# Router of the first 2048 tokens in a pause between two steps of attention, and most of their dispatches in attention's later steps

## The chip, the cores and the metric

The kernel runs on one core of a Trainium2 chip. The metric is the device time of one execution in microseconds (us); lower is better. Engines are named as in the profile: PE (TensorE matmul; PEld its weight loads), DVE (VectorE), ACT (ScalarE), POOL (GpSimd), SP (SyncE, which here only issues DMAs). A DMA that POOL issues with a list of row addresses appears as DMA_INDIRECT on POOL itself.

## The reference, cut to what matters

One transformer block over x of 4 x 1024 x 128 (4096 tokens, in the kernel 32 tiles of 128 tokens) with a modulation by batch:

```python
h = _layernorm(x) * (1 + ca) + sa
x = x + ga * attention(h)            # 16 heads of 8, scores kept where |q - k| <= half, half <= 60
h = _layernorm(x) * (1 + cb) + sb
score = relu(h @ rw1 + rb1) @ rw2 + rb2          # router: 128 -> 512 -> 8
_, topi = top_k(score, 2)                        # two of eight experts for each token
gate = softmax(where(mask(topi), score, -inf))
out = sum over e of gate[:, e] * (relu(h @ W1[e] + b1[e]) @ W2[e] + b2[e])
x = x + gb * out
```

Attention of a tile needs only keys within 60 tokens of it. Everything behind attention is done token by token.

## The kernel before, in words

The program is written out for each engine by hand; every engine runs its own list in order and waits on semaphores. There is no scheduler.

**Preparation** (0 to 43 us): first layer norm, modulation, projections q, k, v.

**Attention** (43 to 255 us) runs 32 steps, one for each tile of 128 tokens. A step has four groups of scores. For each group PE makes the scores (`scores`, L1055), DVE takes row maxima (`maxima`, L1093), ACT takes exponentials (L1026, four per group, each with a read of its sum) and DVE transposes them (`turn`, L1101; the last group's transpose, `turn_last`, L925, stands in the next step). PE then multiplies with the values (`weighted`, L899), one step behind. POOL's list for step t (`turn` in `attend_gpsimd`) is: half of the spread queries of step t + 2 (`queries`, qbd, L338), the spread of the softmax denominators (`denominators`, rsp, L937), the other half of the queries, and the residual sum of the tile before (`residual`, xg L868 and x_all L872). DVE takes the moments of the finished tile for the second layer norm (`moment`, `aggregated`). From step 12 on POOL also refines 1/sqrt(var) of a finished batch of eight tiles by Newton steps (`refined`) and modulates its rows (`group_modulated`, four operations for a group of four tiles, result in h_all).

**Router** (255 to 330 us). The tokens form eight groups of 512 (`NG`). For each group PE turns the rows (`turned_rows`, L1478), makes four hidden blocks (`hidden`, L1485), four partial score products (`partial`, L1492) and their sum (`summed`, L1500). ACT copies and rectifies between them (`turned` L1537, `rectified` L1549, `partials` L1543). DVE adds the bias (`token_scores`, L1425), picks two experts (`choose_both`, 12 operations) and turns ranks into places (`place`), after PE has counted the tokens before each (`ranked`, L1508 and L1510). Choice and places go by parts of tiles, `PARTS = ((0, 4), (4, 8), (8, 16), (16, 24), (24, 32))`. At the head of this stage DVE refines and modulates what POOL hasn't: `last_refined` for the last batch and `last_modulated` for groups 6 and 7.

**Dispatch.** For each tile and each of the two choices POOL issues one DMA_INDIRECT that writes the 128 rows of h_all (576 bytes each) to their places in a DRAM tensor xs, sorted by expert (`dispatch`, L1614): 64 in all, each followed by a small MEMSET on POOL (`breath`, L1656). The last part's dispatches alternate with scatters, two to one.

**Experts** (330 to 513 us) run 72 tiles of 128 sorted rows. DVE builds four lists of which rows and which expert a tile has (`listed`, lists of tiles 0 to 7, 8 to 23, 24 to 39, 40 to 71). SP loads a tile's rows (hg, L1584) once its list stands and all dispatches of batches up to the list's number have landed (`d_x[k]`). PE transposes them (L1927), multiplies up (L1935) and down (L1943); DVE copies weights and rows (`first_matrix` L1793, `gathered` L1798, L1801) and adds the bias (`result`, ys, L1809); ACT rectifies (L1700); POOL scatters the result rows back to token order (`scatter`, L1647). In turns 0 to 5 DVE also has list 2 and the last part's choice; in turns 10 to 15 list 3.

**End** (513 to 537 us): the two results of each token are fetched, weighted, added and stored.

What sets the order around the change is the order of the text in these functions:

```python
                for t in range(NT):           # attend_gpsimd
                    turn(t)
                    ...
                    if t >= 1:
                        residual(e, (t - 1) // 2, (t - 1) % 2)
                sent = 0                      # route_gpsimd
                for p, (first, end) in enumerate(PARTS):
                    routed(e, p)
                    for r in range(2 * first, 2 * end):
                        dispatch(e, r // 2, r % 2)
                        breath()
```

## Time and profile before

| | |
|---|---|
| median of 3 runs | 537.14 us (531.41 to 538.80) |
| profiled execution | 538.34 us, its span 536.5 us |
| PE busy | 453.1 us (84% of the span) |
| DVE busy | 378.4 us (71%) |
| POOL busy | 369.7 us (69%) |
| ACT busy | 349.0 us (65%) |
| mean granted clock of TensorE | 0.927 |

The profile is of one execution. About 1.8 us of its time lie outside the span. All stage times below are us from the span's start. A busy share is an average over stages that have different limits: what a change in one stage is worth is read from that stage.

### The profile page before, as it was taken

To read this page: it belongs to the slowest core of one execution; us is meant where nothing else is said; L and a number is where in the kernel's file an instruction comes from. 1 tells how busy PE (TensorE), PEld (TensorE's weight loads), DVE (VectorE), ACT (ScalarE), POOL (GpSimd) and SP (SyncE) were. 2 spreads that over 40 slices of the span, in tenths; PEclk is the share of its full clock that TensorE was granted. 3 is DMA by queue.
4 is the path that set the end of the run, shared out by engine and by line. 5 is a ranking of instruction groups with operands and counts; after the bars stand their busy time and mean duration, and the time that the engine had idled before them with its cause. 6 is when DMAs were issued, how large, how long until landed. Compare 5 with 4: busy or idle time off the path is not lost.

```text
span 536.5 us, 16755 instructions
## 1 busy us (share of the span) xinstructions
PE 453.1 (84%) x5323; PEld 356.0 (66%) x5323; DVE 378.4 (71%) x1026; ACT 349.0 (65%) x1521; POOL 369.7 (69%) x586
## 2 busy tenths in 40 slices
PE   6998888888888888887929996659668999999977
PEld 5565666666666666665504446658447999999977
DVE  6777999999999999999493565735332554555654
ACT  3668999999999999999523552424023787756800
POOL 6975655556688668764447879875888877777640
PEclk9999999999999999999876996969557999999979
DMA  9351000000000400301311121222211222224446
GB/s 236 83 172 46 13 12 13 13 12 13 14 13 12 111 14 14 91 12 44 99 44 34 51 83 51 81 70 79 91 60 61 80 71 82 69 81 137 133 135 194
DMA packets 61519, 36.54 MB, mean 68 GB/s; under 512 B 25806, under 2 KB 57334, under 8 KB 61306
## 3 DMA queue, kind: packets, MB, share of 16 engines
q1 hardware_dynamic: 55834, 25.83, 18.4%
q0 software_dynamic: 4352, 9.45, 5.2%
q8 instruction: 45, 0.74, 0.6%
q10 hardware_dynamic: 1248, 0.20, 0.2%
q14 instruction: 40, 0.33, 0.2%
HBM read 20.56 MB, written 14.88 MB: 66 GB/s over the span
## 4 chain that ended last, share of the span: by engine, by line
PE 35%; DVE 22%; ACT 21%; issue 12%; another core or an unknown queue 5%; POOL 2%; DVEq 2%; ACTq 0%; POOLq 0%
ACT pr L1026 20%; PE pAm L1935 9%; DVE nmax L1093 8%; PE pAm L1485 5%; PE pSpm L1943 5%; PE pScm L1943 4%; PE pScm L1255 2%; DVE oT L947 1%; PE pScm L1500 1%; DVE w1t L1793 1%; DVEq L1552 1%; PE pm L767 1%; DVE stat L1337 1%; PE pSpm L1492 1%
## 5 line engine op out<-in xcount | busy, mean ns | idle before, releaser
L1026 ACT ACTIVATE pr<-pS,nmax 128x136 f32<-128x136 f32 x512 | 185.5, 382 | 13.4 <-DVE nmax L1093 13.2
L1700 ACT ACTIVATE act<-pAm,w1t 128x128 f32<-128x128 f32 x288 | 82.6, 377 | 85.4 <-PE pAm L1935 41.2
L1026 ACT ACTIVATION_READ_ACCUMULATOR pr<-pS,nmax 128x1 f32 x512 | 108.8, 212 | 0.0
L1935 PE MATMUL pAm<-hgT,w1t 128*128 128x128 f32 x576 | 87.2, 293 | 19.3 <-issue 12.8
L1055 PE MATMUL pS<-kT,qbd 64*128 64x136 f32 x1024 | 93.8, 302 | 1.5 <-ACT pr L1026 1.2
L1935 PEld LDWEIGHTS pAm<-hgT,w1t 128*128 128x128 f32 x576 | 77.6, 206 | 24.7 <-issue 20.0
L1647 POOL DMA_INDIRECT y_scr<-ys,si x72 | 73.2, 1016 | 29.7 <-DVE ys L1809 18.0
L1093 DVE TENSOR_REDUCE nmax<-pS 128x4 f32<-128x544 f32 x128 | 87.6, 685 | 2.1 <-PE pS L1059 1.4
L1101 DVE STREAM_TRANSPOSE prT<-pr 128x640 f32<-128x640 f32 x96 | 81.1, 845 | 8.9 <-ACT pr L1026 0.2
L1055 PEld LDWEIGHTS pS<-kT,qbd 64*128 64x128 f32 x1024 | 68.3, 186 | 14.6 <-ACT pr L1026 1.1
L1614 POOL DMA_INDIRECT xs<-h_all,pos_i x64 | 64.0, 999 | 11.3 <-issue 9.6
L338 POOL TENSOR_TENSOR qbd<-qT,eqd 128x512 f32<-128x512 f32 x64 | 67.6, 1059 | 1.0 <-issue 0.2
L937 POOL TENSOR_TENSOR rsp<-rden,eqt 128x256 f32<-128x256 f32 x33 | 20.5, 621 | 64.4 <-DVE rden L931 61.4
L899 PE MATMUL pO<-prT,vbd 128*32 128x32 f32 (+3 forms) x2048 | 62.4, 253 | 0.0
L899 PEld LDWEIGHTS pO<-prT,vbd 128*32 128x32 f32 x2048 | 47.1, 146 | 19.6 <-issue 19.2
L1793 DVE COPY w1t<-w_all 128x644 f32 x72 | 40.4, 561 | 20.4 <-issue 10.4
L1656 POOL MEMSET unread<- 128x240 f32 x128 | 45.7, 357 | 0.1
L1943 PE MATMUL pScm<-w_all,act 128*128 x288 | 42.1, 285 | 3.7 <-issue 3.3
L1943 PE MATMUL pSpm<-w_all,act 128*128 x288 | 42.2, 289 | 1.6 <-issue 1.6
L920 PE MATMUL pRF<-wcg,oT 128*128 128x128 f32 x68 | 16.5, 324 | 29.4 <-DVE oT L947 28.6
L1943 PEld LDWEIGHTS pScm<-w_all,act 128*128 128x128 f32 x288 | 37.5, 200 | 4.8 <-issue 4.8
L1943 PEld LDWEIGHTS pSpm<-w_all,act 128*128 128x128 f32 x288 | 38.0, 202 | 3.4 <-issue 3.4
(304 smaller groups left out, 716.4 us busy)
## 6 DMA issues: line engine op xcount, KB each, us to landing
hg<-xs SPq DMA_DIRECT2D x72, 72.0 KB
vbd<-v_scr SPq DMA_DIRECT2D x132, 16.0 KB, 1.7
v_scr<-h_all SPq DMA_DIRECT2D x8, 256.0 KB, 2.3
h_all<-y_scr SPq DMA_DIRECT2D x8, 256.0 KB, 3.1
w_all<-y_scr SPq DMA_DIRECT2D x8, 256.0 KB, 5.0
x_all<-in_L_attn_x SPq DMA_DIRECT2D x3, 512.0 KB, 6.1
w_all<-in_L_ffn_W SPq DMA_DIRECT2D x2, 768.0 KB, 4.9
w_all<-in_L_ffn_W SPq DMA_DIRECT2D x3, 512.0 KB, 5.1
```

Source lines behind the costliest of these rows:

```text
L338: e.tensor_tensor(qbd[u][:, 4 * a:4 * a + 4, :].rearrange("p q (h t) -> p q h t", h=NH8), qT[:, bass.ds(t * P + 4 * a * QT, 4 * QT)].rearr ...
L899: mm = e.matmul(pO[32 * hg:32 * hg + 32, lo * QB:(hi + 1) * QB], strided(values, hg, [[HG, QB]]), strided(prT[w][:, hg // 2, 0:1], 2 * WIN ...
L1026: e.activation(pr[:, n, to:to + SPAN], scored(j, gi)[:, lo:lo + SPAN], ACT.Exp, bias=nmax[:, k:k + 1], scale=-1.0, accum_out=rs[u][:, k:k ...
L1055: e.matmul(scored(j, gi)[:, n * BANK + f * SPAN:n * BANK + (f + 1) * SPAN], qbd[j % RING][of_head, 2 * gi + f, :], kT[of_head, first:first ...
L1093: e.tensor_reduce(strided(nmax[:, 0:1], 2 * gi, [[QN, 2], [1, 2]]), strided(scored(j, gi)[:, 0:1], 0, [[BANK, 2], [SPAN, 2], [1, SPAN]]), ...
L1101: e.transpose(rows_of(prT[u], gi), rows_of(pr, gi)).then_inc(v_tr.sem, 1)
L1614: e.indirect_dma_start(out=xs, out_offset=bass.IndirectOffsetOnAxis(ap=pos_i[:, k, n:n + 1].bitcast(U32), axis=0), in_=h_all[:, n, :], in_ ...
L1647: e.indirect_dma_start(out=y_scr, out_offset=bass.IndirectOffsetOnAxis(ap=si[:, j:j + 1].bitcast(U32), axis=0), in_=ys[j % R // 2][:, j % ...
L1700: e.activation(ac(u)[:, k, :], pU[u % W][:, k, :], ACT.Relu, bias=w1t[u // 2 % 4][:, u % 2, FF + D + k:FF + D + k + 1]).then_inc(a_up.sem, 1)
L1793: e.tensor_copy(w1t[u // 2 % 4][:, u % 2, :], w1_all[:, bass.ds(x_, 1), :].rearrange("p a f -> p (a f)")).then_inc(v_w.sem, 1)
L1935: mm = e.matmul(pU[u % W][:, k, :], w1t[u // 2 % 4][:, u % 2, k * P:(k + 1) * P], hgT[u // 2 % 4][:, u % 2, :], start=True, stop=True)
L1943: mm = e.matmul(pY[u // 2 % 2][:, u % 2, 0:D], ac(u)[:, k, :], w2_all[:, bass.ds(x_ * FF + k * D, D)], start=k == 0, stop=k == FC - 1)
```

## The change

The router of groups 0 to 3 (tiles 0 to 15, `G1 = 4`) is taken out of the router stage and put ahead of attention step 20 (`FIRST = NT // 2 + 4`) on PE, ACT, DVE and POOL. Since the buffers of the router stage don't exist during attention, these groups use halves of kT and qT, and staging tiles of the preparation, and another PSUM bank for their scores. Parts 0 to 2 are chosen and placed there; the ranking of part 2 follows on PE behind step 20. POOL issues 28 of these tiles' 32 dispatches inside its turns 20 to 31: three a turn up to turn 27, one a turn from 28 on, without breaths. The last four, and those of parts 3 and 4, stay behind attention. Refinement of batches 1 and 2 moves from POOL to DVE (`batch_refined`, between steps). POOL modulates groups 2 and 3 in the pause and groups 4 and 5 in turns 28 to 31. Behind attention DVE makes lists 0 and 1 before it takes the scores of group 4. The last part is ranked in turn 5 of the experts and not 9, and list 3 follows in turns 6 to 11. Two scatters come ahead of the last part's dispatches. Weight loads on SP wait until the pause's last partial product.

```diff
+            FIRST = NT // 2 + 4
                     if s in LOADED:
+                        e.wait_ge(t_sp, G1)
                         load_weights(e, *LOADED[s])
+                def send(t, k):
+                    if t < FIRST or sent[0] == NT or k and t >= NT - 4:
+                        return
+                    if sent[0] == 2 * PARTS[NP1 - 1][0]:
+                        routed(e, NP1 - 1)
+                    dispatch(e, sent[0] // 2, sent[0] % 2)
+                    sent[0] += 1
                     denominators(e, t // 2, t % 2)
+                    send(t, 0)
                     if t + 2 < NT:
                         queries((t + 2) // 2, t % 2, t + 2, 1)
+                    send(t, 1)
                 for t in range(NT):
+                    if t == FIRST:
+                        first_half_gpsimd(e)
                     turn(t)
...
                         residual(e, (t - 1) // 2, (t - 1) % 2)
+                    send(t, 2)
+                    if t >= NT - 4:
+                        e.wait_ge(v_gs, 3)
+                        for k in range(2 * (t - NT + 4), 2 * (t - NT + 5)):
+                            group_modulated(e, 4 + k // 4, k % 4)
                     if n >= 0 and n % TPB == TPB - 1:
+                        if n // TPB in (1, 2):
+                            batch_refined(e, n // TPB)
                         kept(e)
                         e.sem_inc(v_gs, 1)
+                    if 2 * i + u == FIRST:
+                        summed(e, G1 - 1)
+                        e.wait_ge(v_rt, NP1 - 1)
-            RANKED = 9
+            RANKED = 5
+            SOON = 2
-            BEHIND = {0: 6, 5: 8, 6: 10, 7: 12}
+            BEHIND = {0: 6}
+            def first_half_tensor(e):
+                i, u = (FIRST - 1) // 2, (FIRST - 1) % 2
+                e.wait_ge(d_rw, 64)
+                e.wait_ge(v_k, 3)
+                a_e.wait(e, i, u)
+                turned_rows(e, 0)
+                v_o.wait(e, i, u)
+                a_r.wait(e, i, u)
+                a_x.wait(e, i, u, back=1)
+                for g in range(G1):
+                    group_of_router(e, g, 0, G1)
+                partial(e, G1 - 1)
+            def first_half_vector(e):
+                token_scores(e, 0)
+                choose_both(e, 0)
+                token_scores(e, 1)
+                place(e, 0)
+                choose_both(e, 1)
+                token_scores(e, 2)
+                place(e, 1)
+                token_scores(e, 3)
+                choose_both(e, 2)
+            def first_half_gpsimd(e):
+                e.wait_ge(v_gs, 2)
+                for k in range(8):
+                    group_modulated(e, 2 + k // 4, k % 4)
+                routed(e, 0)
+                routed(e, 1)
+                for r in range(NT - 4, NT):
+                    dispatch(e, r // 2, r % 2)
+                    breath()
-                for p, (first, end) in enumerate(PARTS):
+                for p in range(NP1, len(PARTS)):
-                token_scores(e, 0)
-                choose_both(e, 0)
-                place(e, 0)
-                token_scores(e, 1)
-                choose_both(e, 1)
-                place(e, 1)
                 all_listed(0)
-                token_scores(e, 2)
-                token_scores(e, 3)
-                choose_both(e, 2)
+                all_listed(1)
                 token_scores(e, 4)
-                place(e, 2)
-                all_listed(1)
```

PE's list between steps 19 and 20 (pO<-prT are the products with the values, pS the scores, pRF<-wcg the projection). Before:

```order
L899 MATMUL pO<-prT,vbd 32x64 x4
L899 MATMUL pO<-prT,vbd 32x32 x4
L1055 MATMUL pS<-kT,qbd 128x136 x4
L1059 MATMUL pS<-masks,rep 128x272 x2
L920 MATMUL pRF<-wcg,oT 128x128
```

With the change, from the end of step 19 to the first rows of group 0's router, where the remaining 30 rows follow:

```order
L902 MATMUL pO<-prT,vbd 32x64 x4
L902 MATMUL pO<-prT,vbd 32x32 x4
L1538 MATMUL pTm<-ident,h_all 128x128 x8
L1545 MATMUL pAm<-modr,rw_sb 128x512 x4
L1538 MATMUL pTm<-ident,h_all 128x128 x4
L1545 MATMUL pAm<-gated,rw_sb 128x512 x2
L1552 MATMUL pSpm<-kT,rw2p 32x512 x4
```

and from its last partial product into step 20:

```order
L1552 MATMUL pSpm<-qT,rw2p 32x512 x4
L1083 MATMUL pS<-kT,qbd 128x136 x4
L1087 MATMUL pS<-masks,rep 128x272 x2
L1560 MATMUL pXm<-sel,scp_w 128x8 x4
L923 MATMUL pRF<-wcg,oT 128x128
```

Four router groups now stand between two rows that followed each other; nothing of step 20 stands among them but its first group of scores.

POOL's list for one late turn, from denominators to the next denominators. Before, turn 27 (L338 queries, L868 and L872 residual):

```order
L937 TENSOR_TENSOR rsp<-rden,eqt 128x256
L338 TENSOR_TENSOR qbd<-qT,eqd 128x512
L868 TENSOR_TENSOR xg<-x_all,gacv_bc 128x128
L872 TENSOR_TENSOR x_all<-xg,xa 128x128
L338 TENSOR_TENSOR qbd<-qT,eqd 128x512
L937 TENSOR_TENSOR rsp<-rden,eqt 128x256
```

With the change, turns 20 to 27:

```order
L940 TENSOR_TENSOR rsp<-rden,eqt 128x256
L1723 DMA xs<-h_all,pos_i 34816x144
L340 TENSOR_TENSOR qbd<-qT,eqd 128x512
L1723 DMA xs<-h_all,pos_i 34816x144
L871 TENSOR_TENSOR xg<-x_all,gacv_bc 128x128
L875 TENSOR_TENSOR x_all<-xg,xa 128x128
L1723 DMA xs<-h_all,pos_i 34816x144
L340 TENSOR_TENSOR qbd<-qT,eqd 128x512
```

One dispatch now stands behind the denominators, one behind the queries and one behind the residual.

## Rows read from the trace of the kernel before

**Rows 1.** Busy time by stage (stretch, length, then engines, PEclk, DMA share, GB/s)
```profile
43.20:254.90 211.70, 181.04 (x3458) 132.21 (x3456) 201.12 (x378) 198.14 (x1090) 138.28 (x222) 1.00 0.13 27
254.90:329.80 74.90, 58.50 (x327) 30.38 (x325) 43.78 (x169) 31.18 (x51) 51.62 (x77) 0.82 0.20 61
329.80:420.00 90.20, 67.23 (x412) 59.61 (x413) 38.96 (x145) 29.88 (x108) 73.72 (x113) 0.75 0.24 72
420.00:500.00 80.00, 80.00 (x720) 80.00 (x719) 43.47 (x127) 56.38 (x201) 60.08 (x87) 1.00 0.34 99
```

**Rows 2.** Timeline at the router's start (start, duration, engine, line, operation, [idle before])
```profile
254.56 1.09 PE L1478 MATMUL pTm<-ident,h_all 128*128 128x128 f32 x4
...
255.69 0.60 ACT L1537 ACTIVATE h2T<-pTm 128x512 f32<-128x512 f32 x1 [0.74 <-PE pTm L1478]
```

**Rows 3.** Timeline, PE's rows of two router groups in sequence
```profile
298.43 1.06 PE L1492 MATMUL pSpm<-act,rw2p 128*32 128x512 f32 x8
...
299.42 1.99 PE L1485 MATMUL pAm<-h2T,rw_sb 128*128 128x512 f32 x4
...
302.54 0.95 PE L1500 MATMUL pScm<-sel,scp 128*128 128x8 f32 x8
...
304.38 1.06 PE L1492 MATMUL pSpm<-act,rw2p 128*32 128x512 f32 x8
```

**Rows 4.** Timeline, DVE: first and last operation of list 0; of a choice
```profile
294.42 0.16 DVE L1733 TENSOR_TENSOR cnt<-run,basec 128x8 f32<-128x8 f32 x1
...
299.18 0.17 DVE L1783 TENSOR_TENSOR used<-used,most 128x8 f32<-128x8 f32 x1
...
315.97 0.22 DVE L1437 TENSOR_REDUCE m<-score 128x8 f32<-128x64 f32 x1
...
318.81 0.23 DVE L1452 TENSOR_TENSOR ohb<-oh 128x64 bf16<-128x64 f32 x1
```

**Rows 5.** Timeline, DVE's refinement and modulation at the router's start, beside POOL
```profile
264.47 0.68 DVE L1399 TENSOR_SCALAR var<-mv 128x8 f32<-128x8 f32 x1
...
268.69 1.29 POOL L1391 TENSOR_TENSOR h_all<-h_all,modbc 128x512 f32<-128x512 f32 x1
...
268.87 1.13 DVE L1406 TENSOR_TENSOR newt<-newt,var 128x8 f32<-128x8 f32 x1
...
279.04 0.69 DVE L1421 TENSOR_TENSOR h_all<-h_all,modbc 128x512 f32<-128x512 f32 x1
```

**Rows 6.** Timeline, PE's long wait and the end of the router
```profile
282.64 0.21 PE L1508 MATMUL pXm<-ohb,upper 128*128 128x32 bf16 x1 [10.90 <-DVE ohb L1452]
...
282.80 2.06 PE L1485 MATMUL pAm<-h2T,rw_sb 128*128 128x512 f32 x2
...
326.07 0.19 DVE L1425 TENSOR_TENSOR score<-pScm,rb_bc 128x32 f32<-128x32 f32 x1
...
329.79 3.62 PE L1935 MATMUL pAm<-hgT,w1t 128*128 128x128 f32 x16 [2.81 <-DVE hgT L1798]
```

**Rows 7.** Timeline of POOL: a modulation inside turn 26; turn 27 and the next denominators
```profile
219.91 1.27 POOL L1393 TENSOR_TENSOR h_all<-h_all,modbc 128x512 f32<-128x512 f32 x1
...
222.47 0.62 POOL L937 TENSOR_TENSOR rsp<-rden,eqt 128x256 f32<-128x256 f32 x1 [0.27 <-DVE rden L931]
...
229.35 0.62 POOL L937 TENSOR_TENSOR rsp<-rden,eqt 128x256 f32<-128x256 f32 x1 [3.18 <-DVE rden L931]
```

**Rows 8.** Timeline of POOL, dispatches behind attention
```profile
385.15 0.97 POOL L1614 DMA_INDIRECT xs<-h_all,pos_i  x1 [0.17 <-issue]
...
386.61 0.98 POOL L1614 DMA_INDIRECT xs<-h_all,pos_i  x1 [0.16 <-issue]
```

**Rows 9.** Timeline of the experts while POOL dispatches
```profile
375.67 0.47 PE L1943 MATMUL pSpm<-w_all,act 128*128 x2 [0.37 <-issue]
...
395.70 0.42 DVE L1809 TENSOR_TENSOR ys<-pSpm,w1t 128x256 f32<-128x256 f32 x1 [13.33 <-remote]
```

**Rows 10.** DMA queues, 372 to 402 us (queue, kind: packets, MB, share)
```profile
q8 instruction: 1, 0.02, 0.2%
```

More of the change, by code:

```diff
@@ L190, in build @@
         ohb = [sb(f"ohb{p}", [P, end - first, NE], BF16) for p, (first, end) in enumerate(PARTS)]
-        run = sb("run", [P, NE])
+        run = [sb(f"run{p}", [P, NE]) for p in range(len(PARTS))]
         posg = sb("posg", [P, TPB, NE])
@@ L1044, in scores @@
                         e.wait_ge(a_k, NG)
+                    if 2 * i + u == FIRST and gi < NS:
+                        first_half_left(e, (HG * j + gi) % NS)
                     if gi >= NS:
@@ L1132, in attend_vector @@
                 for t in range(NT):
+                    if t == FIRST:
+                        first_half_vector(e)
                     step(t // 2, t % 2, t % SPANS)
+                    if t == FIRST:
+                        place(e, NP1 - 1)
                     between(t)
@@ L1279, in pPre_of, with pSc_of, h2T_of, scp_of @@
             def pPre_of(p):
-                bank = pX if p < len(PARTS) - 1 else pSc
+                bank = pX if NP1 <= p < len(PARTS) - 1 else pSc
                 place_of = bank[:, 0, P:P + (TPB + 1) * NE]
                 return place_of.rearrange("p (t k) -> p t k", k=NE)
+            def pSc_of(g):
+                return whole(pX if g < G1 else pSc)
+            def h2T_of(g):
+                return ((modr_w, gated_w) if g < G1 else h2T)[g % 2][:, :]
+            def scp_of(g):
+                return ((wmod_sb, scp_w) if g < G1 else scp)[g % 2][:, 0:GRP]
+            def act_of(g):
+                if g < G1:
+                    return (kT, qT)[g % 2][:, 0:FC * GRP].rearrange("p (k t) -> p k t", k=FC)
+                return act[g % 2][:, :, :]
             def modulated_rows(e, g):
@@ L1484, in hidden @@
                     e.wait_ge(a_a2, FC * (g - 1) + k + 1)
-                e.matmul(whole(pA[k]), rw1_sb[:, k * P:(k + 1) * P], h2T[g % 2][:, :], start=True, stop=True).then_inc(t_a2, 1)
+                e.matmul(whole(pA[k]), rw1_sb[:, k * P:(k + 1) * P], h2T_of(g), start=True, stop=True).then_inc(t_a2, 1)
             def partial(e, g):
@@ L1491, in partial @@
                 for k in range(FC):
[L1492 removed]
+                    mm = e.matmul(whole(pSp)[QB * k:QB * k + QB, :], rw2p[:, k, :], act_of(g)[:, k, :], start=True, stop=True, skip_group_check=True)
                 mm.then_inc(t_sp, 1)
@@ L1499, in summed @@
                 for n in range(4):
-                    mm = e.matmul(whole(pSc)[:, n * NE:(n + 1) * NE], scp[g % 2][:, n * P:(n + 1) * P], sel[:, :], start=True, stop=True)
+                    mm = e.matmul(pSc_of(g)[:, n * NE:(n + 1) * NE], scp_of(g)[:, n * P:(n + 1) * P], sel[:, :], start=True, stop=True)
                 mm.then_inc(t_sc, 1)
@@ L1512, in ranked, with group_of_router @@
                 mm.then_inc(t_rk, 1)
-            def group_of_router(e, g):
-                if g + 1 < NG:
+            def group_of_router(e, g, first, end):
+                if g + 1 < end:
                     turned_rows(e, g + 1)
                 hidden(e, g, 0)
-                if g >= 4:
-                    summed(e, g - 2)
-                if g == 6:
-                    ranked(e, 2)
                 hidden(e, g, 1)
-                if g >= 1:
+                if g > first:
                     partial(e, g - 1)
-                if g in (2, 3):
+                if first == 0 and g >= 2:
@@ new lines, in first_half_left, with first_half_scalar @@
+            def first_half_left(e, bank):
+                if bank == 0:
+                    e.wait_ge(a_t2, G1)
+                    e.wait_ge(v_sc, G1)
+                else:
+                    e.wait_ge(a_a2, FC * G1)
+            def first_half_scalar(e):
+                turned(e, 0)
+                for g in range(G1):
+                    if g + 1 < G1:
+                        turned(e, g + 1)
+                    rectified(e, g, 0)
+                    rectified(e, g, 1)
+                    if g >= 1:
+                        partials(e, g - 1)
+                    rectified(e, g, 2)
+                    rectified(e, g, 3)
+                partials(e, G1 - 1)
@@ L1536, in turned @@
                     e.wait_ge(t_a2, FC * (g - 1))
-                e.activation(h2T[g % 2][:, :], whole(pT), ACT.Copy).then_inc(a_t2, 1)
+                e.activation(h2T_of(g), whole(pT), ACT.Copy).then_inc(a_t2, 1)
             def partials(e, g):
@@ L1542, in partials @@
                     e.wait_ge(t_sc, g - 1)
-                e.activation(scp[g % 2][:, :], whole(pSp), ACT.Copy).then_inc(a_sp, 1)
+                e.activation(scp_of(g), whole(pSp), ACT.Copy).then_inc(a_sp, 1)
             def rectified(e, g, k):
@@ L1548, in rectified @@
                 e.wait_ge(t_a2, FC * g + k + 1)
-                e.activation(act[g % 2][:, k, :], whole(pA[k]), ACT.Relu, bias=rb1_sb[:, k:k + 1]).then_inc(a_a2, 1)
+                e.activation(act_of(g)[:, k, :], whole(pA[k]), ACT.Relu, bias=rb1_sb[:, k:k + 1]).then_inc(a_a2, 1)
             def expert(e, i, u):
@@ L1631, in route_gpsimd @@
                 residual(e, NI, 0)
-                for k in range(2, 8):
-                    group_modulated(e, 4 + k // 4, k % 4)
                 v_tr.wait(e, NI - 1, 1)
@@ L1657, in breath @@
                     breaths[0] += 1
+                for r in range(NT - 4, NT):
+                    dispatch(e, r // 2, r % 2)
+                    breath()
                 sent = 0
-                for p, (first, end) in enumerate(PARTS):
+                for p in range(NP1, len(PARTS)):
+                    first, end = PARTS[p]
+                    if p == len(PARTS) - 1:
+                        for _ in range(SOON):
+                            scatter(sent)
+                            breath()
+                            sent += 1
                     routed(e, p)
@@ L1677, in route_scalar @@
                 projected(e, NI, 0)
-                turned(e, 0)
+                turned(e, G1)
                 to_rows(e, NI, 0)
-                for g in range(NG):
+                for g in range(G1, NG):
                     if g + 1 < NG:
```

50 lines of the change are left out of this document (30 added, 20 removed).

## The prediction

> **What bounds the kernel now.** The table of busy time by stage comes first [rows 1]; its columns after the length are PE, PEld, DVE, ACT, POOL, clock, DMA share and GB/s. In attention DVE and ACT are busy 201 and 198 of 212 us, so its 32 steps of 6.6 us have no hole for anything on these two. POOL has one: 138 of 212. A turn of POOL, seen in its timeline, ends 3.2 us before the next denominators are due [rows 7]: 6.88 us from one rsp to the next, of which 3.7 are work. The router stage has no full engine (58 of 75 on PE). It is a chain, and its worst link is one wait of PE of 10.9 us for the choice on DVE [rows 6]. In the experts PE sets the pace where all goes well: 720 rows in the 80 us from 420 on, 9.0 a us, none idle. Ahead of that, 329.8 to 420, it did 412 rows in 90.2 us [rows 1]. At 9.0 a us they take 45.8 us, so **44 us are lost there**. About 7 belong to turns 0 to 5, in which DVE also has list 2 and the last choice (about 1.2 each). The other 37 are stalls: two PE products that took 0.47 us after 0.37 idle on "issue", where the good stretch has nine rows a us, and DVE rows that waited 13.3 us for a signal from elsewhere [rows 9]. All this lies where POOL issues indirect DMAs every 1.46 us (385.15 to 386.61, of which the DMA_INDIRECT is 0.97 and the rest a small MEMSET and gaps [rows 8]).
>
> The sum is made against the profiled execution (538.3 us, 1.2 above the median).
>
> **(a) The pause, +34.** From the last exponential of step 19 to the first of step 20, ACT does only router work and DVE too. In order: PE turns group 0 and ACT copies it, 1.7 us (254.56 to 256.29 [rows 2]). The eight products of its hidden blocks take 4.0 (1.99 for four [rows 3]). Group 2 must wait for its modulation: DVE's refinement of batch 1 is 14 operations of 0.17 and a gap, 2.9; POOL's four operations of 1.27 [rows 7] make 5.1 more. That is 8.0 against 5.7 on PE, so 2.3 of wait. Three groups more at the period of the old stage, 298.43 to 304.38 or 5.95 [rows 3], are 17.9. Parts 0 and 1 are ranked in it (0.9). The last partial and its copy are 2.4, the sum 1.0 [rows 3]. Part 2's choice has 3.1 (315.97 to 319.04 [rows 4]), the score ahead of it 0.2. Step 20's first maxima, 0.7, end it. Together 34.2. The maxima of step 20 stand behind all of DVE's choice in the order of its list, so no part of the choice is hidden. Bounds: 31, if the modulation is early and choice overlaps; 45, if the clock is at its lower level for the pause, where two products take 2.06 in place of 1.0 [rows 6, 3].
>
> **(b) The router behind attention, -28.** Before it was 74.9 (254.9 to 329.8 [rows 1]). Now only groups 4 to 7 are left, and groups 4 and 5 are modulated in turns 28 to 31. DVE starts its refinement at 264.5 as before, since the last residual sets that. It took 8.9 us up to 273.3, as some operations of 0.17 took 1.13 while POOL modulated beside them [rows 5]. POOL now has nothing there: I take 5. The modulation of group 6 is four of 0.69, 2.8, so PE may turn it at 272.3, and group 7 is done at 275.1. Then DVE makes lists 0 and 1, 4.9 each (294.42 to 299.35 [rows 4]), and takes the scores of group 4 at about 285.2. PE has gone on to group 6 and waits there for that read. From it there are two periods of 5.95 and a ranking to the last scores at 297.4. The old kernel needed 3.7 from its last scores to the first product of an expert (326.07 to 329.79 [rows 6]); with place 3 a bit more, 4.3. The experts start 301.7 on the old scale, 46.8 behind attention: -28. Bounds -25 (refinement as slow as before) and -31 (lists partly beside PE's work of group 6).
>
> **(c) Attention's later steps, +8.** In turns 20 to 27 POOL has 3.65 of its own and three dispatches of 0.97 with a gap of 0.17 [rows 8], 3.45: 7.1 a turn against steps of 6.6. That is +0.5 for eight turns, 4, less about 1 of slack at the start: +3. What is late then is the spread of softmax denominators; ACT and DVE wait for the products behind them. The refinement of batch 2 now lies on DVE, which is full there: +3 to 4 (2.9 alone; 8.9 beside POOL's reads [rows 5]). Turns 28 to 31 have one dispatch and two modulation rows of 1.27: 3.65 + 1.15 + 2.5 = 7.3, +1.2 in all after slack. Bounds: 0 (the denominators absorb it, as 3.2 us idle stood there [rows 7]) and +20 (below).
>
> **(d) The experts, -6.** Before they took 183: 139 at PE's pace and 44 lost. Turns 0 to 5 cost the same 7; list 3 comes in turns 6 to 11, where before the stalls hid it: 4. The stalls I tie to the time in which POOL issues indirect DMAs without a pause beside the experts. Before this was about 78 us, and cost 37: 0.47 a us. Now part 3 is sent from 298 to 322 and part 4 with its scatters to 360: 58 us, which gives 27. I take 26. The sum is 139 + 7 + 4 + 26 + 1 for the two scatters = 177. Bounds: 0 for the stalls, -32; 37 as before, +5. Lists don't gate: tile 24 isn't due before 349, and the last dispatch lands by 360.
>
> **Sum:** 538.3 + 34 - 28 + 8 - 6 = 546.3; less 1.2 to the median, **545 us**. The pause buys back nearly its price and no more: the same four groups cost 34 in a place where all else stands still, and save 28 in the other. The gain can come from the experts alone, with 28 of the 64 dispatches gone from there.
>
> **Rivals.**
>
> *B, faster: the stalls go.* If the loss of 37 comes from dispatches that gate loads (SP waits for a whole batch before it may load hg, then all arrive together) rather than from POOL's pace, it goes with the 28 dispatches. For it: it ended at about 416, some 15 us behind the last dispatch, and batch 3 landed last at 401. Against: PE rows of a tile whose data were there also crept [rows 9]. With 5 left in place of 26 the time is 524; with 0, 519. Place it at 521. Chance 0.28.
>
> *C, slower: the stalls move into attention.* 28 dispatches of 1.15 are 32 us of POOL's issuing. At the same 0.47 lost for each such us, attention loses 15 more than POOL's own time, since DVE and ACT have no slack [rows 1]: 560. It decides from +3: a turn from 20 to 27 of over 7.5 us. Against: the dispatches behind denominators, queries and residual are apart, so POOL does not issue them back to back. Chance 0.15.
>
> *D, slower: the clock.* PE stood 10.9 us and its products came at 2.06 for two afterwards [rows 6]; the stage has a mean clock of 0.82, attention 1.00 [rows 1]. In the pause PE waits 2 to 3 us at three places. At the lower level (1.2 GHz) for half of it, 555. Chance 0.05.
>
> *E, slower: the stall is tied to a place in the program.* PE creeps with "issue" as the releaser, as if its instructions came late. Then it recurs at the same tiles with all its 37: 556. Against: the queue that brings instructions had a single packet in these 30 us [rows 10]. Chance 0.07.
>
> The Trainium skill (Runtime: NRT & Kernel Launch, section Instruction fetch mechanics) says that an engine's instructions are fetched in blocks of 16 KiB while it works through the last, and that the cost is mostly hidden; the one packet agrees, and by that page E would add nothing. The Trainium skill (SBUF — State Buffer, section Who interferes with whom) says that a VectorE operation with two inputs in SBUF and a GpSimd operation that reads SBUF exclude each other; by that, batch 2's refinement in the middle of attention could cost up to the slow case. The trace agrees in 264 to 273, where only some of the operations were slow.
>
> **Chances and range.** The forecast has 0.45, with a range of its own of 538 to 552: pause 31 to 37, attention +3 to +12, stalls 18 to 33. A change under 2% is about what a measurement of this kernel can't tell from none: 526.4 to 547.9. Of the forecast's 0.45, 0.34 lie within, 0.11 above. B gives 0.24 to faster and 0.04 to within. C, D and E give 0.25 to slower and 0.02 to within. Faster 0.24, within 0.40, slower 0.36. The range that holds 8 in 10 is 520 to 564: below it lies half of B, above it the far end of C.
>
> **What would show it.** Right: ACT's gap between steps 19 and 20 about 34; rsp to rsp in turns 20 to 27 about 7.1; first L1935 row (new line number) 47 behind attention's end; the clock at 1.00 in the pause; PE rows of the first 60 us of the experts at less than 9 a us and "issue" among their releasers, ending with the last dispatch. Wrong: stalls gone with POOL still dispatching (B); turns 20 to 27 at 7.5 or more (C); a lower clock in the pause (D); the stall at the same tiles as before (E).

## Result, and the profile of the changed kernel

| | before | changed |
|---|---|---|
| median, four runs each | 534.27 us (531.28 to 538.80) | 555.79 us (550.69 to 557.04) |
| profiled execution, its span | 538.34, 536.5 | 555.90, 554.1 |
| ratio | | 1.038 (95% interval 1.027 to 1.049) |
| mean granted clock | 0.927 | 0.911 |

The changed kernel is slower by 3.8%. The forecast was 545 us. Its wide range of 520 to 564 holds the result, its own range of 538 to 552 does not, and the likeliest case (within 2%) did not come. Busy time by stage, changed kernel (stretch, length, then PE, PEld, DVE, ACT, POOL, clock, DMA share, GB/s), to set beside [rows 1]. The stretches are all attention with its pause, the pause, steps 20 to 31, the router behind attention, the experts' first 79 us, a later stretch of the experts:

```profile
48.70:306.00 257.30, 215.85 (x3584) 150.61 (x3581) 218.28 (x461) 214.33 (x1112) 169.11 (x234) 0.95 0.12 30
176.00:214.00 38.00, 32.19 (x224) 16.84 (x216) 15.93 (x74) 19.57 (x47) 12.32 (x16) 0.91 0.13 37
214.00:306.00 92.00, 73.95 (x1276) 53.67 (x1277) 81.07 (x164) 75.31 (x408) 75.89 (x93) 0.89 0.18 48
306.00:351.60 45.60, 31.33 (x196) 15.86 (x196) 27.55 (x114) 16.38 (x27) 14.60 (x24) 0.80 0.23 66
351.60:431.00 79.40, 62.89 (x337) 54.02 (x338) 34.11 (x133) 22.28 (x81) 58.31 (x91) 0.73 0.23 69
431.00:500.00 69.00, 69.00 (x622) 69.00 (x621) 37.39 (x109) 50.74 (x182) 51.13 (x74) 1.00 0.26 76
```

The pause fills PE to 32 of 38 us, DVE and ACT only to 16 and 20. In steps 20 to 31 no engine is over 81 of 92, where DVE was at 95% over all of attention before. The experts are as before: 9.0 PE rows a us in the good stretch, 337 rows in 79 us ahead of it. By marks that both timelines have (first exponential; denominators of steps 0, 19, 20 and the last; first expert product; last ys; end), the two executions split so:

| part | before | changed | difference | forecast |
|---|---|---|---|---|
| preparation, to the first exponential | 44.6 | 49.9 | +5.3 | none |
| steps 0 to 19 | 125.0 | 124.9 | -0.1 | 0 |
| denominators 19 to 20 (the pause) | 6.9 | 40.3 | +33.4 | +34 |
| denominators 20 to the last | 79.1 | 91.9 | +12.8 | +8 |
| to the first expert product | 74.2 | 44.7 | -29.5 | -28 |
| experts, to the last ys | 185.0 | 181.8 | -3.2 | -6 |
| end | 21.7 | 20.7 | -1.0 | 0 |

The sum is +17.6 (before rounding), that of the two spans.

**The pause.** ACT's last exponential of step 19 and first of step 20, and on DVE the first score, the last choice and the maxima behind it:

```profile
179.55 0.38 ACT L1050 ACTIVATE pr<-pS,nmax 128x136 f32<-128x136 f32 x1
...
214.16 0.37 ACT L1050 ACTIVATE pr<-pS,nmax 128x136 f32<-128x136 f32 x1 [5.31 <-DVE nmax L1131]
```
```profile
193.33 0.19 DVE L1485 TENSOR_TENSOR score<-pXm,rb_bc 128x32 f32<-128x32 f32 x1 [10.74 <-PE pXm L1560]
...
210.06 0.19 DVE L1485 TENSOR_TENSOR score<-pXm,rb_bc 128x32 f32<-128x32 f32 x1 [3.91 <-PE pXm L1560]
...
213.33 0.16 DVE L1513 TENSOR_TENSOR gates<-m 128x8 f32<-128x8 f32 x1
213.41 0.72 DVE L1131 TENSOR_REDUCE nmax<-pS 128x4 f32<-128x544 f32 x1
```

Four scores at 193.3, 199.4, 205.3 and 210.1: twice the period of 6 us from [rows 3], then 4.8. The last exponential and the next are 34.6 us apart.

**Turns 20 to 27.** POOL from one denominators row to the next:

```profile
239.21 0.62 POOL L940 TENSOR_TENSOR rsp<-rden,eqt 128x256 f32<-128x256 f32 x1
240.00 1.01 POOL L1723 DMA_INDIRECT xs<-h_all,pos_i  x1 [0.17 <-issue]
241.04 1.06 POOL L340 TENSOR_TENSOR qbd<-qT,eqd 128x512 f32<-128x512 f32 x1
242.26 1.01 POOL L1723 DMA_INDIRECT xs<-h_all,pos_i  x1 [0.17 <-issue]
243.30 0.46 POOL L871 TENSOR_TENSOR xg<-x_all,gacv_bc 128x128 f32<-128x128 f32 x1
243.93 0.46 POOL L875 TENSOR_TENSOR x_all<-xg,xa 128x128 f32<-128x128 f32 x1 [0.17 <-POOL xg L871]
244.60 0.99 POOL L1723 DMA_INDIRECT xs<-h_all,pos_i  x1 [0.22 <-PE pS L1087]
245.62 1.07 POOL L340 TENSOR_TENSOR qbd<-qT,eqd 128x512 f32<-128x512 f32 x1
246.64 0.62 POOL L940 TENSOR_TENSOR rsp<-rden,eqt 128x256 f32<-128x256 f32 x1
```

No gap over 0.22 is left and the denominators wait for nothing, where 3.18 us stood idle before [rows 7]: POOL sets 7.43 us a turn. In turn 21, of 8.98 us, PE's granted clock falls to 0.50 for 4 us, and POOL waits 1.52 us for the denominators; eight score products take 1.28 there and 0.73 later:

```profile
223.68 1.28 PE L1083 MATMUL pS<-kT,qbd 64*128 64x136 f32 x8
...
228.35 0.73 PE L1083 MATMUL pS<-kT,qbd 64*128 64x136 f32 x8
```
```profile
222.80:227.00 4.20, 4.20 (x64) 3.07 (x64) 2.95 (x4) 3.01 (x17) 3.81 (x6) 0.50 0.05 18
```

Turn 25 takes 8.11 at full clock. In it POOL turns part 2's places into addresses (`routed`), 0.69 us more with the gaps, which no term of the sum had:

```profile
257.01 0.21 POOL L1730 TENSOR_SCALAR h_all<-rank 128x8 f32<-128x8 f32 x1
257.28 0.20 POOL L1731 CAST pos_i<-pos 128x16 int32<-128x16 f32 x1
257.76 1.03 POOL L1723 DMA_INDIRECT xs<-h_all,pos_i  x1 [0.28 <-POOL pos_i L1731]
```
```profile
254.10:262.10 8.00, 5.77 (x110) 4.17 (x110) 6.44 (x13) 6.43 (x36) 6.93 (x10) 1.00 0.16 38
```

Turn 26, where the mean clock is 0.68, still takes 7.41: there POOL hides it.

Turn 27, with the refinement of batch 2 on DVE in it, takes 10.82. POOL waits for it:

```profile
273.89 0.28 DVE L1459 TENSOR_SCALAR var<-mv 128x8 f32<-128x8 f32 x1
...
275.41 1.66 DVE L1464 TENSOR_TENSOR newt<-rstd 128x8 f32<-128x8 f32 x1
...
278.32 0.17 DVE L1470 TENSOR_TENSOR rstd<-rstd,newt 128x8 f32<-128x8 f32 x1
...
280.39 0.62 POOL L940 TENSOR_TENSOR rsp<-rden,eqt 128x256 f32<-128x256 f32 x1 [3.35 <-DVE rden L934]
```

**The preparation.** Its text is the same in both kernels, up to line numbers. One DVE row with two inputs in SBUF, of one element, stood 4.64 us. It started while the second of POOL's four queries rows ran and ended with the fifth row from there, at 38.3. PE then waited 2.68 us, and its clock fell (0.52 from 39.4 to 42.0, 1.00 in the same place before):

```profile
32.57 4.10 POOL L340 TENSOR_TENSOR qbd<-qT,eqd 128x512 f32<-128x512 f32 x4
...
33.67 4.64 DVE L389 TENSOR_TENSOR sc<-sc 1x1 f32<-1x1 f32 x1
...
37.84 0.46 POOL L636 TENSOR_TENSOR wcg<-modbc,wc 128x128 f32<-128x128 f32 x1
...
39.43 1.12 PE L756 MATMUL pQ<-h_all,wqs 128*128 128x512 f32 x1 [2.68 <-DVE qT L396]
```

**The experts.** Late signals are still there (rows of ys that waited 8.83 and 10.45 us on "remote", to set beside [rows 9]), now at the first and at the fifth to seventh ys row (one for two tiles); before it was the sixth to ninth.

```profile
412.06 0.42 DVE L1925 TENSOR_TENSOR ys<-pScm,w1t 128x256 f32<-128x256 f32 x1 [8.83 <-remote]
...
425.32 0.42 DVE L1925 TENSOR_TENSOR ys<-pSpm,w1t 128x256 f32<-128x256 f32 x1 [10.45 <-remote]
```

What the 28 early dispatches leave free on POOL turns into waiting. POOL stands 22.88 us before part 3 for its places and 9.00 before part 4 for its:

```profile
347.60 0.21 POOL L1730 TENSOR_SCALAR h_all<-rank 128x8 f32<-128x8 f32 x1 [22.88 <-DVE pos L1531]
...
385.53 0.20 POOL L1730 TENSOR_SCALAR h_all<-rank 128x8 f32<-128x8 f32 x1 [9.00 <-DVE pos L1531]
```

In the kernel before it had no wait at part 3 and 6.54 at part 4. Part 4's last dispatch moved from 400.0 to 419.1.

### The profile page after: what moved, and what is told of

It is laid out like the page before. It is cut to its first block, busy times and chain, and to the rows that moved or that the text cites. A ratio compares the mean times of both kernels' runs of the same rounds, so it can differ in the third digit from the quotient of the medians.

```text
span 554.1 us, 16734 instructions
## 1 busy us (share of the span) xinstructions
PE 466.7 (84%) x5323; PEld 363.2 (66%) x5323; DVE 381.2 (69%) x1054; ACT 350.2 (63%) x1521; POOL 354.4 (64%) x530
## 4 chain that ended last, share of the span: by engine, by line
PE 41%; ACT 18%; DVE 17%; issue 11%; POOL 7%; another core or an unknown queue 4%; DMA 1%; DVEq 1%; SPq 0%; ACTq 0%; POOLq 0%
ACT pr L1050 15%; PE pAm L2041 10%; DVE nmax L1131 5%; PE pAm L1545 5%; PE pScm L2049 5%; PE pSpm L2049 5%; POOL xs L1723 2%; PE pS L1083 2%; PE pO L902 2%; ACT act L1816 2%; PE pScm L1300 2%; POOL qbd L340 2%; PE pSpm L1552 1%; DMA x_all<-in_L_attn_x 1%
## 5 line engine op out<-in xcount | busy, mean ns | idle before, releaser
L2041 PE MATMUL pAm<-hgT,w1t 128*128 128x128 f32 x576 | 90.5, 298 | 13.2 <-issue 6.2
L1083 PE MATMUL pS<-kT,qbd 64*128 64x136 f32 x1024 | 98.0, 312 | 1.5 <-ACT pr L1050 1.2
L2041 PEld LDWEIGHTS pAm<-hgT,w1t 128*128 128x128 f32 x576 | 79.2, 208 | 19.5 <-issue 14.6
L1083 PEld LDWEIGHTS pS<-kT,qbd 64*128 64x128 f32 x1024 | 71.6, 194 | 16.4 <-ACT pr L1050 1.9
L902 PE MATMUL pO<-prT,vbd 128*32 128x32 f32 (+3 forms) x2048 | 64.7, 259 | 6.5 <-DVE prT L928 6.5
L902 PEld LDWEIGHTS pO<-prT,vbd 128*32 128x32 f32 x2048 | 48.6, 147 | 27.4 <-issue 26.8
L923 PE MATMUL pRF<-wcg,oT 128*128 128x128 f32 x68 | 17.2, 336 | 24.9 <-DVE oT L950 22.7
L1087 PE MATMUL pS<-masks,rep 64*128 64x272 bf16 x256 | 37.1, 282 | 0.0
```

Source lines behind the costliest of these rows:

```text
L902: mm = e.matmul(pO[32 * hg:32 * hg + 32, lo * QB:(hi + 1) * QB], strided(values, hg, [[HG, QB]]), strided(prT[w][:, hg // 2, 0:1], 2 * WIN ...
L1083: e.matmul(scored(j, gi)[:, n * BANK + f * SPAN:n * BANK + (f + 1) * SPAN], qbd[j % RING][of_head, 2 * gi + f, :], kT[of_head, first:first ...
L2041: mm = e.matmul(pU[u % W][:, k, :], w1t[u // 2 % 4][:, u % 2, k * P:(k + 1) * P], hgT[u // 2 % 4][:, u % 2, :], start=True, stop=True)
```

## Experiments

One thing has to be known first: the same kernel before has a median of 534.4 us beside one group of runs and of 514.6 and 514.7 beside the two others. The twelve runs came in three groups of four, each group on a chip of its own, and each run is compared with the kernel before of its own group. Each chip was met only once, so what belongs to the chip and what to its condition at that time can't be told apart. In the two groups at 515 no trace has a DVE row that waited over 1.5 us on "remote"; in the group at 534, and in the two first profiles, all have them. I call these a **quiet** and a **stalling** chip. On a quiet chip the kernel before has times and no trace, and the changed kernel has neither as it stands.

**Both kernels again, for traces beside each other** (a stalling chip). No edit.

> The kernel before, unchanged, for a trace on this chip. On the chip of the last four runs its median was 514.6 us, against 537.1 where both were profiled first. If the stalls of the experts belong to the chip or its moment and not to the program, its trace there has no DVE row that waits over 2 us on a late signal, and PE does its 9 rows a us from about 380 on; at the end POOL's scatters, spaced 1.46 us by the MEMSETs, are the last to finish. If they belong to the program, the stretch 372 to 418 creeps here too. Ratio to itself 1.00.

> The changed kernel, unchanged. From its parts: pause 34, router behind attention 29 shorter, last twelve steps 12 longer, so 17 behind at the first expert; without stalls, POOL's chain of dispatches and scatters sets the end, and it has 28 fewer of them behind attention. Theory POOL (the end is POOL's, no stalls): the experts take 5 to 12 us less than in the kernel before, 520 to 527 where before is 515. Theory stalls (the experts' loss is as on the first chip): 533 to 556.

Measured: 533.4 against 534.4 for the kernel before, ratio 0.999 (0.996 to 1.002), and 548.9 for the changed one, ratio 1.027 (1.019 to 1.035). The parts repeat: first exponential 44.3 and 49.2; pause 39.9 between denominators; from denominators 20 to the last 79.0 and 91.9; the router behind attention 74.4 and 44.7; experts 178.4 and 177.5. The change gives the experts 1 to 3 us on a stalling chip and not 6. The text for the stalling case (533 to 556) holds the changed kernel.

**No dispatch in attention, and two a turn** (a quiet chip).

```diff
 def send(t, k):
-    if t < FIRST or sent[0] == NT or k and t >= NT - 4:
+    if True:
```

with all 32 dispatches behind attention, and for two a turn, with twelve behind it

```diff
+    if t < FIRST or sent[0] == NT or k == 2 or k and t >= NT - 4:
```

> The changed kernel, but with no dispatch inside attention: all 32 of tiles 0 to 15 are issued behind it. My theory from the two traces: POOL's turns 20 to 27 set the 7.4 us steps, so the last twelve steps come back from 91.8 us (first to last denominators of turns 20 to 32) to about 83, with only the refinement of batch 2 above the old 79.1. Behind attention 28 dispatches of 1.46 us are added ahead of part 3, whose first dispatch then stands some 50 us behind attention and not 43; the experts lose about as much to stalls as before (35 to 40 us) instead of 30. Sum: 556 - 9 + 7 = about 554, no clear difference from the changed kernel. Rival B (dispatches in attention are what helps the experts): above 562. Rival C (dispatches in attention cost more than the turns): below 547.

> The changed kernel with two dispatches a turn in turns 20 to 27 and not three; 20 go in attention, 12 behind. My theory: POOL has 3.65 + 2 x 1.18 = 6.0 a turn, under the 6.57 of DVE and ACT, so the turns fall back to 6.6 us and attention gets 7 us shorter, for 8 more dispatches behind it that are hidden (part 3 isn't chosen before 43 us behind attention): 549. Rival: the turns stay near 7.4, since a dispatch delays the denominators wherever it stands: 556.

The numbers of these two expectations are for a chip like that of the first profiles; what holds here is their distances. Measured: 537.9 with none, ratio to the kernel before 1.046 (1.040 to 1.053); 519.0 with two a turn, 1.009 (1.005 to 1.013). From denominators 20 to the last it is 83.9 us with none, 85.2 with two, 91.7 with three (on a quiet chip, next but one below). So in attention the third dispatch costs 6.5 us and the first two 1.3: it is the length of POOL's turn that counts, not the dispatch. (The kernel with three is the repaired one at the end of this section; its whole time, 518.8, is that of the kernel with two, whose preparation was 2.6 us longer in its trace.) Of the run with none I expected no clear difference to the changed kernel, and that was wrong: it is the slowest of these, though its attention is the shortest. The rival of that text, that the dispatches in attention are what helps the experts, is the one that this chip bears out. Its part 4 starts at 383.1 and not at 370.4, and POOL then never catches up: the last ys stands at 500.1, POOL's last scatter 13.6 us behind it.

DVE's last ys row, and POOL's last row:

```profile
500.07 0.41 DVE L1926 TENSOR_TENSOR ys<-pScm,w1t 128x256 f32<-128x256 f32 x1
```
```profile
513.67 0.97 POOL L1754 DMA_INDIRECT y_scr<-ys,si  x1 [0.30 <-issue]
```

In this run the end belongs to POOL's chain of dispatches and scatters, one each 1.46 us at best, and dispatches taken out of its head are worth their time: with two a turn part 4 starts at 366.0, 17.2 us sooner, and the span is 17.4 shorter.

**The kernel before without the MEMSETs, twice** (both times a quiet chip). `breath()` returns at once.

> The kernel before without any of the small MEMSETs, so dispatches follow at 1.15 us. Theory S: stalls get deeper while POOL dispatches (more lost a us) but the time of it is shorter by a fifth: 537 to 550. Theory G: batches land up to 20 us sooner and the loss shrinks: 520 to 528. Theory P: 535.

> The kernel before without MEMSETs once more, since the chips differ. Theory S (where the stalls exist they grow with POOL's rate): on a chip where the kernel before takes some 535, its stalls get deeper but POOL is through sooner, 530 to 545, ratio 0.99 to 1.02. On a chip without stalls (before at 515) it is 0.975 again.

Measured: 502.0, ratio 0.975 (0.971 to 0.979), and 501.3, ratio 0.976 (0.971 to 0.980). Neither run met stalls, so the expectation for a stalling one is untried. In the first text theory S had no gain and fell for this chip; theory G (batches land sooner) had the right side, but the trace shows another reason: POOL keeps up. Its last scatter is 2.5 us behind the last ys. In the groups of POOL's scatters from 362 to 515 us (count, busy, mean ns, idle before and what ended it), with the changed kernel on a quiet chip (the repaired one below), then the kernel before without MEMSETs:

```profile
L1754 POOL DMA_INDIRECT y_scr<-ys,si x72 | 72.8, 1011 | 12.9 <-issue 10.6 <-DVE si L1917 1.1 <-DVE ys L1925 1.1
```
```profile
L1647 POOL DMA_INDIRECT y_scr<-ys,si x72 | 73.2, 1017 | 29.5 <-issue 14.6 <-DVE ys L1810 13.0 <-DVE si L1802 1.8
```

With MEMSETs POOL waits 1.1 us in all for results to scatter, it is hardly ever free; without them 13.0. The two kernels differ by the change as well, so this is a sign and no proof; that the time is POOL's rests on the 12.6 and 13.5 us that the MEMSETs' removal gives, and on the longer MEMSETs below.

**The changed kernel without MEMSETs; and with two a turn, without them** (a stalling chip).

> The changed kernel without the small MEMSETs. Theory POOL: POOL's chain behind attention gets 0.3 us shorter for each of some 100 indirect DMAs, but here PE already sets the end, so only 3 to 8 us are gained. Theory PE (the changed kernel's experts are at PE's pace from the start): nothing is gained, ratio to the changed kernel 1.00. With stalls on this chip: slower or equal, as stalls get deeper.

> The changed kernel with two dispatches a turn and without the MEMSETs. Both gains add: attention 7 shorter by the trace of the run with two a turn, the POOL chain shorter: 508 to 515 where the kernel before is 515 and the one without MEMSETs 502. If the pause costs as much as it saves behind attention, it can't get below the kernel before without MEMSETs (502).

Measured: 553.4, ratio to the kernel before 1.035 (1.026 to 1.043), and 555.4, 1.037 (1.030 to 1.045), where the changed kernel of the same group had 1.027. Nothing is gained; by the intervals none of the three can be told from another. In the traces the experts take 183.4 and 186.2 us without MEMSETs and 177.5 with them. (The removal was tried in the kernel before on quiet chips and in the changed one on a stalling chip, so chip and kernel changed together.) Busy time in stretches of 5 us of the first of the two, while POOL issues one indirect DMA each 1.26 us:

```profile
385.00:390.00 5.00, 3.16 (x21) 2.72 (x20) 0.86 (x4) 0.87 (x4) 3.78 (x5) 0.91 0.23 75
390.00:395.00 5.00, 1.41 (x4) 0.76 (x3) 3.90 (x11) 0.00 (x0) 3.78 (x5) 0.50 0.21 66
395.00:400.00 5.00, 0.82 (x3) 0.58 (x2) 0.00 (x0) 0.00 (x0) 3.78 (x5) 0.50 0.17 52
400.00:405.00 5.00, 0.74 (x2) 0.58 (x2) 0.00 (x0) 1.14 (x4) 3.78 (x5) 0.50 0.20 70
405.00:410.00 5.00, 1.66 (x8) 1.84 (x9) 0.95 (x3) 1.05 (x5) 0.73 (x1) 0.50 0.14 47
```

PE does two or three products in 5 us, each with up to 2.43 idle on "issue":

```profile
398.89 0.37 PE L2042 MATMUL pAm<-hgT,w1t 128*128 128x128 f32 x1 [1.73 <-issue]
401.02 0.37 PE L2042 MATMUL pAm<-hgT,w1t 128*128 128x128 f32 x1 [1.75 <-issue]
403.82 0.37 PE L2042 MATMUL pAm<-hgT,w1t 128*128 128x128 f32 x1 [2.43 <-issue]
```

POOL stops between 405 and 410 and PE starts again in that stretch. The same stage with POOL issuing each 1.46 us has 49 rows in 15 us on the same chip (changed kernel), and 121 rows on a quiet one (repaired kernel):

```profile
395.00:410.00 15.00, 10.39 (x49) 7.74 (x48) 4.75 (x15) 3.42 (x12) 13.35 (x22) 0.79 0.32 99
```
```profile
380.00:395.00 15.00, 14.02 (x121) 13.36 (x121) 9.76 (x31) 9.05 (x33) 13.34 (x21) 1.00 0.36 112
```

POOL is as busy in both (13.35 and 13.34). So POOL's issuing alone does not make stalls; the chip, or its condition, has to be one that has them. That they deepen with POOL's rate is not shown. The two traces without MEMSETs lost the most (70 and 69 rows in the 25 us of part 4's issuing) and the changed kernel with them less (165 in 32.6), but the kernel before, on the same chip with the same pace of 1.46 us, had hardly any there:

```profile
364.00:399.50 35.50, 31.31 (x263) 29.78 (x262) 20.47 (x69) 17.72 (x66) 31.57 (x45) 1.00 0.32 94
```

Its stalls came behind part 4's dispatches, from 400 to 445, where POOL issued scatters alone.

**A longer MEMSET** (all three on a quiet chip): in the kernel before from part 4 to the end, in it for part 4 alone, and in the changed kernel for parts 3 and 4.

```diff
-unread = sm("unread", [P, 240])
+unread = sm("unread", [P, 900])
...
-e.memset(unread[:, :], 0.0)
+e.memset(unread[:, 0:900 if 48 <= breaths[0] < 72 else 240], 0.0)   # part 4 alone
```

> The kernel before with a longer MEMSET behind each dispatch and scatter of the last part and behind later scatters (128 x 900 in place of 128 x 240), nothing else. Theory S (the stalls of PE and the late signals come from POOL issuing indirect DMAs at 1.46 us without a pause): at a pace of 2.1 us the stretch 372 to 418 gets back PE rows at near 9 a us; PE then waits only for the last batch's landing at about 418: 15 to 20 us faster, about 520. Theory G (the loss is waiting for batches to land): the last batch lands 15 us later, so the time is 10 to 15 us longer, about 550. Theory P (place in the program): the creeping stays at the same tiles, 540 to 550.

> The kernel before with the longer MEMSET (128 x 900) only behind the last part's 16 dispatches and 8 scatters; later scatters at the old pace. With stalls on this chip, theory S: the stretch in which these are issued loses at most 0.1 us of PE work a us in place of 0.4 to 0.5, part 4 is through at about 415; ratio 0.97 to 1.00. Theory P (not POOL's pace): the same stalls, ratio 1.02. Without stalls on this chip: POOL is the last to finish and 24 x 0.6 = 14 us are added, ratio 1.025.

> The changed kernel with the longer MEMSET behind the 42 dispatches and scatters of parts 3 and 4. With stalls, theory S: no DVE row of the experts waits over 3 us on a late signal; PE's 30 us of stalls shrink to under 10, less 6 to 10 us for part 4 landing later: 530 to 540 where the changed kernel is 549 to 556. Theory P: 560. Without stalls: 25 us more of POOL work, the kernel 5 to 20 us slower than the changed one would be.

Measured: 555.4, ratio 1.078 (1.074 to 1.083); 527.1, 1.025 (1.020 to 1.030), as expected for a chip without stalls; 544.2, 1.059 (1.053 to 1.066), which is 25.4 over the repaired kernel of the same chip, 4.3 of it in the preparation. The first text of the three was written for a chip at 535 and had 550 at most for any theory; it was wrong in not seeing POOL as the bound. Each is POOL's chain made longer: in the first, ys rows follow each other at 4.12 us a pair, two times POOL's 2.06. None of them could test whether a slower pace removes stalls, since there were none to remove. What causes the stalls stays open.

**The two-input rows of the preparation written with one tensor** (changed kernel, a quiet chip).

```diff
-step("_i", e.tensor_tensor(sc[:, 15:16], dst, val, ALU.is_gt))
+step("_i", e.tensor_scalar(sc[:, 15:16], dst, val, None, ALU.is_gt))
...
-step("_i", e.tensor_tensor(dst, dst, sc[:, 15:16], ALU.subtract))
+step("_i", e.tensor_scalar(dst, dst, sc[:, 15:16], None, ALU.subtract))
```

> The changed kernel with the two TENSOR_TENSOR rows of 1 element in the preparation (the rounding of the window's width, two inputs in SBUF) written as TENSOR_SCALAR with a scalar from SBUF; nothing else. In five of six traces of kernels with the change the first of them took 4.64 us beside POOL's four queries rows (0.98 in the others), PE then stood 2.68 us and in three of the five its clock fell. If two-input DVE rows are kept out while POOL reads: each of the new rows takes 0.14 to 0.2, PE has no gap of 2.68 us there, the first exponential comes at 43 to 44.5 and not at 46 to 50, and the kernel is 2 to 6 us faster than the changed one. If the wait is for something else, the row stays at 4.6.

Measured: 518.8, ratio to the kernel before 1.006 (1.003 to 1.010). The rows now take 0.20:

```profile
33.88 0.20 DVE L389 TENSOR_SCALAR sc<-sc 1x1 f32<-1x1 f32 x1
34.12 0.20 DVE L391 TENSOR_SCALAR sc<-sc 1x1 f32<-1x1 f32 x1
```

PE has no gap there, and the first exponential is at 43.9. The row of 4.6 us stands in six of the seven other traces of kernels with the change and in one of the six without; the one with none in attention lacks it, the kernel before with its slower part 4 has it. In these seven the first exponential is at 46.1 to 49.9, in the six others at 44.0 to 44.6. Which of the two comes out is thus not settled by whether the change is in, and what decides it, and why it came more often with the change, stays open; DVE's start behind POOL's is 1.09 to 1.11 us in traces of both kinds. The changed kernel itself did not run on a quiet chip, so its own gain by the repair there isn't measured; by the marks it is 2 to 6 us.

The repaired kernel is also the changed kernel's best trace on a quiet chip: denominators 20 to the last 91.7, experts from 345.2 to 496.3, 151 us, against 182 on the first chip. Its last dispatch of part 4 goes at 404.1; part 4 had started at 370.4, 2.7 us behind the second early scatter. Without the change part 4 starts at 361.6 on a quiet chip (the kernel with longer MEMSETs from part 4 on, first exponential at 44.5). So the 28 dispatches moved forward don't bring part 4 forward: POOL stands 22.8 us before part 3 for the places of its tiles, is busy with part 3 from 342.0 on, and waits 0.5 for part 4's places. Both choices are bound to the end of the router and to DVE's first turns, and the pause puts these later.

## Why the prediction was right or wrong

- **What bounds the kernel**: right for attention (DVE and ACT) and for the chip of that profile. It took for a property of the program what belongs to a chip or its condition: on a quiet one the kernel before takes 515 us, no trace there has stalls, and taking the MEMSETs off POOL gives 13 us. I read [rows 9] as POOL's doing alone. The chip is a part of it; whether POOL's rate is another is open.
- **(a) the pause, +34**: 33.4, and 34.6 on ACT. Right in its terms: 8.0 us to the modulation of group 2, where PE turned group 2 at 188.1, 8.6 behind the last exponential's start; periods of 6.0, 6.0 and 4.8; 4.1 from the last score to the exponentials. The clock was 0.91 in this stretch and not 1.00 as named there; it was at 0.50 near the start, where the eight products took 5.2 and not 4.0, hidden behind the wait for group 2's modulation.
- **(b) the router behind attention, -28**: -29.5, inside its bounds. The score of group 4 came 30.3 us behind attention's last exponential, as worked out.
- **(c) the later steps, +8**: +12.8, the first term that was mis-sized. The step that failed is POOL's turn. The three dispatches lengthen it from 3.70 to 7.43, 1.24 each and not 1.15 (1.01 with a gap of 0.17 to 0.22, and the row behind starts later), and the 1 us of slack did not show: eight turns of 7.4 against 6.6 cost 6.9, where the sum had 3. The refinement was right (3.4 over a turn of 7.4; between 2.4 and 4.0 in the other traces). The lower clock in turn 21, which I had as a rival for the pause alone, gives 1.5, and part 2's places in turn 25 give 0.7, which I had left out. Turns 28 to 31 gave 0.3 where the sum had 1.2. Rival C's 560 from stalls inside attention fell, though its sign (a turn of over 7.5) was missed only narrowly: no late signal stands in these turns, and with two dispatches a turn the steps are 6.6.
- **(d) the experts, -6**: -3.2, and -1 to -3 in both pairs of traces. The side was right. Ahead of 431 us, 42 us are lost (79.4 less 337 rows at 9.0 a us), where the sum had 37 and the kernel before 44; "0.47 lost a us of issuing" was a rate fitted to one execution. The second pair gives less in both kernels (178). Rival B (stalls gone) fell on the chip of the forecast. What it named, waiting for POOL's chain, is real on a quiet chip: there, dispatching nothing in attention costs 19 us against two a turn. Rival E fell: on quiet chips nearly the same programs have no stalls, and between two executions of the kernel before on stalling chips the longest wait of a ys row went from the seventh (13.3 us) to the fourteenth (9.05 us). The Trainium skill (Runtime: NRT & Kernel Launch, section Instruction fetch mechanics) calls the fetch mostly hidden; the traces fit that, for each has 45 fetches of 16 KiB, and they take 0.9 to 1.7 us on both kinds of chip.
- **Not in the sum: +5.3 in the preparation.** Half of what was missing (the forecast for the profiled execution was 546.3, it took 555.9). No term stood for a stage that the change does not touch. The row was in the trace of before, as four of 0.98, 0.99, 1.02 and 0.38 us for one element, and the 4.64 of the other outcome is thirty times the 0.15 that such a row takes alone. The Trainium skill (SBUF — State Buffer, section Who interferes with whom) says that a DVE operation with two SBUF inputs and a GpSimd one that reads SBUF exclude each other; the trace agrees in kind, and the repair's 0.20 fits it. The page speaks of waiting for an instruction; here DVE stood through five of POOL's.

The large misses have one sign: -0.8 in (a) and -1.5 in (b) against +4.8 in (c), +1.8 in (d) with the end, and +5.3. The wide range holds the result by luck: its upper part stood for C, D and E, and none of them came; 5.3 us of preparation and a mis-sized (c) led there instead. The bottom line stands as argued on a stalling chip: the pause costs what it saves (+33.4, -29.5), and the dispatches cost attention more than they give the experts. On a quiet chip the first two dispatches a turn pay (19 us against none); whether the third does isn't shown.

**No version of the change beat the kernel before.** What did, on a quiet chip and twice, is the kernel before without MEMSETs (0.975). On a stalling chip it was not run; the changed kernel did not gain by it there.

## What to carry to other kernels

A piece of work moved into a pause of a stage whose engines are full costs its whole length; it pays only if these engines stand idle in its old place and something behind it gets to start earlier, so look for what the next stage really waits for (here the choice and places of parts 3 and 4, not the first parts' dispatches). Count the turn of a half idle engine to the tenth before adding to it: in attention two dispatches were nearly free, the third cost 6.5 us. Before fitting a theory to stalls in one trace, take a second trace of the same kernel, if possible on another chip.

## What the runs showed of the hardware that I had not expected

- The same kernel before took 515 us on two chips and 534 on another, and most of the difference is in the experts (their first product stands at 325.9, 326.4 and 328.0 in three of the four traces without the change on the faster ones and at 330.7 in the fourth, which has the row of 4.6 us; at 329.3 and 329.8 on the slower): there PE's rows crept and signals came 4 to 15 us late, at times when POOL issued indirect DMAs, though not at all such times. Why one chip does so is open.
- A DVE TENSOR_TENSOR on one element stood 4.64 us through five rows of POOL that read SBUF; a TENSOR_SCALAR with its scalar from SBUF in the same place took 0.20.
- A gap of 2.68 us on PE was followed, in some executions and not in others, by a stretch at 1.2 GHz (granted clock 0.52 from 39.4 to 42.0 in the changed kernel's first trace); with it the first exponential stood at 48.3 to 49.9, without it at 46.1 and 46.6.
